# Deformable-convolution block: values and their transposes in three places, two PSUM banks for transposed values, one for the shuffle

## What is computed

```python
x = x + _L0_conv_ref(_gn(x), L0_conv_W, L0_conv_b)      # 8 groups, 3x3, then per group (channels, pixels) -> (pixels, channels)
x = x + _L1_conv_ref(_gn(x), ...)
# _L1_conv_ref:
out = relu(_bn(_conv1x1(x, conv1_w, conv1_b), ...))       # 512 -> 128 channels
offset = _conv3x3(out, off_w, off_b)                      # 18 channels: dy, dx for 9 taps
out = _deform_conv3x3(out, offset, dconv_w, dconv_b)      # val = v00*wy0*wx0 + v01*wy0*wx1 + v10*wy1*wx0 + v11*wy1*wx1
out = _bn(out, ...)
out = relu(_bn(_conv1x1(out, conv2_w, conv2_b), ...))     # 128 -> 512 channels
```

## Time and profile before

| | us |
|---|---|
| median of 3 runs | 2017.78 |
| lowest and highest run | 2017.04 and 2052.67 |
| the profiled execution | 2034.64 |
| its span, first to last instruction | 2032.8 |
| mean granted TensorE clock in it | 0.910 |
| DMA, mean over the span | 220 GB/s |

### The profile page before, as it was taken

The page is one execution under the profiler, slowest core; times in us unless marked ns, Lnnn a source line. Parts: engine busy times, 40 slices in busy tenths (PEclk is TensorE's granted clock), DMA queues, the critical chain, the costliest instruction groups (busy, mean ns, idle before and its releaser), DMA issues.

```text
span 2032.8 us, 30610 instructions
## 1 busy us (share of the span) xinstructions
PE 1658.7 (82%) x9504; PEld 794.9 (39%) x9504; DVE 1424.5 (70%) x3577; ACT 952.5 (47%) x1411; POOL 1198.0 (59%) x1160
## 2 busy tenths in 40 slices
PE   4888888888888888988887978888888888887555
PEld 2444434344443434434343433434334343433211
DVE  5547678686777778686776857777686777867553
ACT  6645445454545445454543636545354553523221
POOL 0036666665666666665665666666655665666762
PEclk9988889998998989899998989999999998998866
DMA  8267678697786868778686867969687786867774
GB/s 216 63 179 212 201 198 278 193 280 209 216 269 194 268 184 268 220 211 278 204 265 179 263 210 203 292 184 293 190 240 241 218 265 185 250 191 224 221 214 122
DMA packets 161423, 446.68 MB, mean 220 GB/s; under 512 B 26598, under 2 KB 27238, under 8 KB 161254
## 3 DMA queue, kind: packets, MB, share of 16 engines
q0 software_dynamic: 92160, 302.06, 51.0%
q1 hardware_dynamic: 69094, 142.58, 22.2%
HBM read 373.23 MB, written 71.30 MB: 219 GB/s over the span
## 4 chain that ended last, share of the span: by engine, by line
PE 42%; issue 20%; DVE 11%; another core or an unknown queue 10%; ACT 9%; DMA 4%; POOL 3%; SPq 1%; ACTq 0%; DVEq 0%; POOLq 0%
PE bank L820 18%; PE bank L797 7%; PE bank L788 4%; PE bank L805 3%; DVE sb_rows L601 3%; POOL sb_rows L364 3%; PE bank L910 3%; DMA sb_xc<-x 2%; DVE sb_val L609 2%; PE bank L852 2%; ACT sb_split L442 2%; DVE sb_split L641 2%; PE bank L836 2%; ACT sb_norm L429 2%
## 5 line engine op out<-in xcount | busy, mean ns | idle before, releaser
L364 POOL DMA_INDIRECT sb_rows<-table,sb_ridx x1152 | 1194.2, 1037 | 784.1 <-issue 441.6
L820 PE MATMUL bank<-sb_split,sb_wg 128*64 128x512 f16 x4608 | 630.7, 406 | 101.6 <-issue 85.8
L601 DVE SCALAR_TENSOR_TENSOR sb_rows<-sb_rows,sb_frac 128x256 f32<-128x256 f32 x1152 | 500.4, 480 | 186.5 <-DMA sb_rows<-table,sb_ridx 139.4
L820 PEld LDWEIGHTS bank<-sb_split,sb_wg 128*64 128x64 f16 x4608 | 266.2, 114 | 434.8 <-issue 270.7
L609 DVE SCALAR_TENSOR_TENSOR sb_val<-sb_rows,sb_frac 128x128 f32<-128x128 f32 x1152 | 328.7, 347 | 29.1 <-PE bank L788 11.0
L797 PE MATMUL bank<-sb_valT,sb_wd 128*128 128x512 f32 x576 | 342.9, 679 | 7.4 <-issue 7.0
L788 PE MATMUL bank<-sb_eye_sb,sb_val 128*128 128x128 f32 x1152 | 200.9, 300 | 146.7 <-ACT sb_valT L392 72.6
L392 ACT ACTIVATE sb_valT<-bank 128x512 f32<-128x512 f32 x288 | 174.0, 604 | 228.4 <-remote 133.3
L414 ACT ACTIVATE sb_conv_sb<-bank,sb_bias 128x512 f32<-128x512 f32 x128 | 147.0, 1149 | 226.4 <-remote 130.1
L788 PEld LDWEIGHTS bank<-sb_eye_sb,sb_val 128*128 128x128 f32 x1152 | 132.7, 150 | 307.3 <-issue 255.9
L403 ACT ACTIVATE sb_res<-bank,sb_bn_t,sb_bn_s 128x512 f32<-128x512 f32 x128 | 99.5, 778 | 297.4 <-remote 175.6
(11 more groups left out here) (76 smaller groups left out, 1067.4 us busy)
## 6 DMA issues: line engine op xcount, KB each, us to landing
table<-sb_table_sb SPq DMA_DIRECT2D x144, 256.0 KB
sb_xc<-x SPq DMA_DIRECT2D x64, 512.0 KB
sb_xl<-x SPq DMA_DIRECT2D x128, 256.0 KB
out<-sb_xl SPq DMA_DIRECT2D x128, 256.0 KB
sb_rows<-table,sb_ridx POOLq DMA_INDIRECT x1152
sb_rows<-w_group SPq DMA_DIRECT2D x8, 288.0 KB, 9.6
sb_wd<-w_def SPq DMA_DIRECT2D x1, 576.0 KB
sb_w<-w_in SPq DMA_DIRECT2D x1, 512.0 KB
```

Of the source, the lines that this page charges most:

```text
L364: pool.indirect_dma_start(out=rows[:, (c % RING) * PER + i, :], out_offset=None, in_=tables[u % 2], in_offset=bass.IndirectOffsetOnAxis(ap ...
L601: op = nc.vector.scalar_tensor_tensor(r[:, 0:2 * CH], r[:, 2 * CH:4 * CH], frac[:, parity, half * PER + i, k, 0:1], r[:, 0:2 * CH], ALU.mu ...
L820: op = nc.tensor.matmul(pair_ps[half][64 * e:64 * e + 64, :], wg[:, 2 * q + e, k, part * GIN:(part + 1) * GIN], plane(split1[:, 2 * q + e, ...
```

## The change

- `val` and `valT` get three places in place of two (`VALUES`). `value_out` waits for the `deform` of one chunk further back, and VectorE's second interpolation for the transposes of one chunk further back.
- Transposed values alternate between banks 4 and 5. `transpose_values` of chunk c waits for the copy of chunk c-2 in place of c-1.
- Both parts of the shuffle use bank 2. A part waits until the part before it has been added.
- Table tiles alternate between bank 2 and `out_ps`. Tile 0 waits for both parts of the next image's first shuffle, tile 1 for the last `relu_out` of the image before the last; the first `out_conv` of an image waits for the copies of all tiles.

```diff
+    VALUES = 3
...
-        val = sb("val", [128, 2, PER * CH], f32)
-        valT = sb("valT", [128, 2, HALF], f32)
+        val = sb("val", [128, VALUES, PER * CH], f32)
+        valT = sb("valT", [128, VALUES, HALF], f32)
...
-        shuf_ps = (banks[2], banks[5])
+        shuf_ps = banks[2]
...
-        valT_ps = banks[4]
+        valT_ps = (banks[4], banks[5])
         def_ps = banks[6]
         out_ps = banks[7]
+        table_ps = (shuf_ps, out_ps)
...
             def value_out(image, c):
                 act.wait_ge(valT_done, count(CHUNKS, image, c + 1))
-                act.wait_ge(def_done, count(CHUNKS, image, c - 1))
-                nc.scalar.activation(valT[:, c % 2, :], valT_ps[:, :], ACT.Copy).then_inc(val_out, 1)
+                act.wait_ge(def_done, count(CHUNKS, image, c - VALUES + 1))
+                nc.scalar.activation(valT[:, c % VALUES, :], valT_ps[c % 2][:, :], ACT.Copy).then_inc(val_out, 1)
...
-                    nc.scalar.activation(table_sb[:, m % TBUFS, :], shuf_ps[m % 2][:, :], ACT.Copy).then_inc(tile_out, 1)
+                    nc.scalar.activation(table_sb[:, m % TBUFS, :], table_ps[m % 2][:, :], ACT.Copy).then_inc(tile_out, 1)
...
-                    dve.wait_ge(valT_done, count(CHUNKS, image, c - 1))
+                    dve.wait_ge(valT_done, count(CHUNKS, image, c - VALUES + 1))
...
             def transpose_values(image, c):
                 pe.wait_ge(val_done, count(CHUNKS, image, c + 1))
-                pe.wait_ge(val_out, count(CHUNKS, image, c))
+                pe.wait_ge(val_out, count(CHUNKS, image, c - 1))
...
-            def out_conv(image, g):
+            def out_conv(image, g, table):
                 if g == 0:
+                    if table:
+                        pe.wait_ge(tile_out, count(TILES, image + 1, TILES))
                     pe.wait_ge(d_out, count(2, image, 2))
...
             def shuffle(image, q, part):
                 pe.wait_ge(conv_out, count(2 * QUADS, image, 2 * q + 2))
-                pe.wait_ge(mid_done, count(2 * QUADS, image, 2 * q + part - 1))
+                pe.wait_ge(mid_done, count(2 * QUADS, image, 2 * q + part))
...
                 def table_tile(m):
                     if m < 2:
-                        pe.wait_ge(mid_done, count(2 * QUADS, nxt, m + 1) if a2 else count(2 * QUADS, t, 2 * QUADS))
+                        if m == 0:
+                            pe.wait_ge(mid_done, count(2 * QUADS, nxt, 2) if a2 else count(2 * QUADS, t, 2 * QUADS))
+                        else:
+                            pe.wait_ge(relu_done, count(GROUPS, t - 1, 0))
```

More of the change, by code:

```diff
@@ L609, in interpolate @@
                         op = nc.vector.scalar_tensor_tensor(
-                            val[:, c % 2, i * CH:(i + 1) * CH], r[:, CH:2 * CH],
+                            val[:, c % VALUES, i * CH:(i + 1) * CH], r[:, CH:2 * CH],
                             frac[:, parity, half * PER + i, k, 1:2], r[:, 0:CH], ALU.mult, ALU.add)
@@ L650, in add_shuffled @@
                     dst = xl[:, buf, 2 * q:2 * q + 2, part * (HALF // 2):(part + 1) * (HALF // 2)]
-                    nc.vector.tensor_tensor(dst, shuf_ps[part].rearrange("p (e n) -> p e n", e=2), dst, ALU.add)\
+                    nc.vector.tensor_tensor(dst, shuf_ps.rearrange("p (e n) -> p e n", e=2), dst, ALU.add)\
                       .then_inc(mid_done, 1)
@@ L785, in transpose_values @@
                 pe.wait_ge(val_done, count(CHUNKS, image, c + 1))
-                pe.wait_ge(val_out, count(CHUNKS, image, c))
+                pe.wait_ge(val_out, count(CHUNKS, image, c - 1))
                 for i in range(PER):
-                    op = nc.tensor.transpose(valT_ps[:, i * CH:(i + 1) * CH],
-                                             val[:, c % 2, i * CH:(i + 1) * CH], eye_sb[:, :])
+                    op = nc.tensor.transpose(valT_ps[c % 2][:, i * CH:(i + 1) * CH],
+                                             val[:, c % VALUES, i * CH:(i + 1) * CH], eye_sb[:, :])
                 op.then_inc(valT_done, 1)
@@ L796, in deform @@
                     pe.wait_ge(d_out, count(2, image, half))
-                nc.tensor.matmul(def_ps[:, :], wd[:, k * CH:(k + 1) * CH], valT[:, c % 2, :], start=k == 0,
+                nc.tensor.matmul(def_ps[:, :], wd[:, k * CH:(k + 1) * CH], valT[:, c % VALUES, :], start=k == 0,
                                  stop=k == TAPS - 1).then_inc(def_done, 1)
-            def out_conv(image, g):
+            def out_conv(image, g, table):
                 if g == 0:
+                    if table:
+                        pe.wait_ge(tile_out, count(TILES, image + 1, TILES))
                     pe.wait_ge(d_out, count(2, image, 2))
@@ L829, in shuffle @@
                 pe.wait_ge(conv_out, count(2 * QUADS, image, 2 * q + 2))
-                pe.wait_ge(mid_done, count(2 * QUADS, image, 2 * q + part - 1))
+                pe.wait_ge(mid_done, count(2 * QUADS, image, 2 * q + part))
                 if q == 1 and part == 0:
                     pe.wait_ge(tile_out, count(TILES, image - 1, TILES))
-                dst = shuf_ps[part].rearrange("p (e j o) -> p j e o", e=2, o=GIN)
+                dst = shuf_ps.rearrange("p (e j o) -> p j e o", e=2, o=GIN)
                 for jj in range(COLS // 4):
@@ L909, in table_tile @@
                     for i, src in enumerate((h_sb[:, r], dx[:, r], dy[:, r], dxy[:, r])):
-                        op = nc.tensor.transpose(shuf_ps[m % 2][:, i * CH:(i + 1) * CH], src, eye_sb[:, :])
+                        op = nc.tensor.transpose(table_ps[m % 2][:, i * CH:(i + 1) * CH], src, eye_sb[:, :])
                     op.then_inc(tile_done, 1)
@@ L964, in step @@
                     if tail and s in OUT_CONV:
-                        out_conv(t - 1, OUT_CONV[s])
+                        out_conv(t - 1, OUT_CONV[s], b)
                     offsets_and_table(s, 3)
```

## The result

| | before | changed |
|---|---|---|
| median, lowest, highest (us), 4 runs each | 2035.16, 2017.04, 2052.67 | 2047.19, 2046.90, 2057.41 |
| the profiled execution, its span | 2034.64, 2032.8 | 2047.11, 2045.3 |
| mean granted clock in it | 0.910 | 0.914 |

The ratio is 1.016 with an interval of 1.0107 to 1.0213. I had forecast 1996.8 us, 21 us less than the 2017.78 of before, in a range of 1964 to 2038. The changed kernel lies outside it, on the slower side, though still within the 2%. The kernel before took 2017 us twice and 2052 us twice (the table ahead of the prediction has three of these four), and the ratio leaves out the two of 2052 us as executions in a slower state of the chip. So 1.6% rests on two runs of the kernel before; the means over all four and four, 2035.0 and 2049.7 us, are 0.7% apart.

The account below looks back on a forecast made before the run. The prediction took queue handovers, chiefly TensorE's transposes waiting for ScalarE's copy with VectorE ahead, to bound the kernel. Won 39 less lost 18 gave net 21 us, from 2017.78 to 1996.8 us, range 1964 to 2038.

Parts of the forecast that it names:

- won 39: Sum of the gains expected from doubling the bank of the transposed values: 8 + 18 + 8 + 5 us.
- The transposes' wait goes: TensorE's value transposes (L788) would lose their idle time for the copy L392: 59.0 us steady, 72.6 in all.
- Slot 1, won 8: Transposes and part of the offset convolution run inside the gap behind ScalarE's DMA wait: 0 to 18 us, taken 8.
- Slots 7 and 9, won 18: Transposes there wait less, since a group convolution stands between them and `deform`: 8 to 26.8 us, taken 18.
- The merged bank, lost 10 and 4: Shuffle parts wait for VectorE's add: 10 us in slot 11, 4 at the start, nothing in the other four slots.
- Start and end, won 5: Waits for the copy outside the steady stretch, 13.6 us in all, shrink: 0 to 14 us, taken 5.
- The third place for values, nothing: A third place for `val` lets VectorE, already ahead, get further ahead, hidden behind TensorE's work: no time.
- Clock, won 8, lost 4: Closed gaps in slots 7 and 9 give back clock, 0 to 15 us; longer shuffle gaps cost 0 to 10.
- The tiles in `out_ps`, nothing: Table tiles keep their two-bank alternation in bank 2 and `out_ps`: no time; 11 us if cover were gone.
- the rule: A skill's report that a second PSUM buffer gave no further gain (126.6 to 125.5 us); by it, gains about nothing.
- No change: Rival: TensorE passes the transposes and stops at ScalarE's next product; 2012 to 2022 us, say 2017; chance 0.25.
- The slower rival: At the merged shuffle bank, each of five handovers an image shows one VectorE add: about 2060 us; chance 0.15.

Follow-up runs that it names:

- the pair with half the gathers: Kernel before and changed kernel, each with only the first two of four gathers a chunk issued after the first three chunks: 1691.14 and 1685.30 us.
- The pair with half the shuffle: Kernel before without the second part of every shuffle, tiles in bank 2 and `out_ps`, with one or two banks for transposed values: 2034.42 and 2031.68 us.
- three other orders: Two VectorE adds earlier in the changed kernel, 1.0152; in the kernel before, value transposes behind the second convolution, 1.0094, or a ScalarE copy ahead of a ReLU, 0.9981.
- the larger sets: The unedited changed kernel measured again against the kernel before, on two chips: 2037.57 us, ratio 1.0061, and 2031.90 us, ratio 1.0043.
- the earlier pace: Kernel before with GpSimd's wait for the transposes ahead of a chunk's second gather instead of its third: 2017.94 us, ratio 0.9967.

## Why the prediction was wrong

The step that failed is the one from waits to time: "won 39" priced the waits for the copy at their length. Where only the doubling differs and no bank is merged, 79.8 us of these waits went and the time moved by 0.5 us by the means, with a standard error of 3.1, and by 2.7 us by the medians. Term by term:

**The transposes' wait goes** (my first step). Right: 72.6 us to nothing.

**Slot 1, won 8.** Wrong size. The mechanism was named, that the tile stops behind the same DMA, and I still took two thirds of a microsecond a step for it. Measured: 62.7 against 60.9 us in slots 1 and 2, nothing won that stands out of the scatter.

**Slots 7 and 9, won 18.** The gaps before the transposes shrank by 17 us, as counted, but 27.3 us stand before the shuffle of slot 9. I had read there that the add ended 1.4 us ahead, and called four of the five handovers "hidden as long as TensorE doesn't gain more than that". TensorE now stood there up to 5.2 us for the add.

**The merged bank, lost 10 and 4.** This term was mis-sized. The gaps are 13.4 us in slot 11, priced at 10, and 9.2 us in the first 100 us, priced at 4; slots 9 and 16, priced at nothing, have 27.3 and 13.5. What ended with the add is 57.0 us in all (34.2 and 34.5 in the two later traces of the changed kernel). Its effect on the time is smaller than on the waits: the kernel with only that edit has 22.9 us of such waits and is slower by 0.15%, with its interval on both sides of nothing.

**Start and end, won 5.** Not seen. From slot 1 of the last step in the steady stretch to the end it is 388.7 us before and 396.1, 393.0 and 394.1 in three traces of the changed kernel, and 379.7 to 397.4 in six other kernels with one bank. Only the pair with half the gathers shows it clear of that: some 6 us longer, not shorter.

**The third place for values, nothing, since VectorE is ahead.** Here the premise failed. The earlier trace rows gave 2.6 us of waits for the values against 59.0 for the copy, and I took the small number for a lead. A wait that ends last hides how late the others were. With the copy out of the way the values were just behind: 34.6, 44.4 and 30.9 us of waits in three traces, 19.8 before (10.7 to 27.7 in six other kernels with one bank), and 44.6 against 26.2 in the pair with half the gathers. The pair with half the shuffle does not show it (37.3 with one bank, 29.4 with two), so it was not always VectorE that came next.

**Clock, won 8, lost 4.** Not seen: the granted clock was 0.910 before and 0.914, 0.926 and 0.908 in three traces of the changed kernel, its busy TensorE 1670.0, 1645.9 and 1671.5 us against 1658.7.

**The tiles in `out_ps`, nothing.** Right, 0.9993.

**The sum.** Its common error lies under all terms: I took a microsecond of a TensorE wait for a microsecond of time. The runs say that in this kernel it isn't. TensorE with some 40 us less work, VectorE with 222 us less, half the gathers' bytes and three other orders moved the time by -17 to +15 us, far less than what was taken away. What moves it much is GpSimd's gathers: 328 us less with half of them, 195 us more with the same number and no pacing. The page has 1152 of them at 1037 ns with 0.30 us between two, about 1540 us of work, which I passed over because "59%" leaves those 0.30 us out. The timeline of the changed kernel shows a run of eight, with what the others do meanwhile:

```profile
373.25 0.95 POOL L366 DMA_INDIRECT sb_rows<-table,sb_ridx  x1 [2.40 <-remote]
...
379.12 0.60 PE L840 MATMUL bank<-sb_eye_sb,sb_conv_sb 128*128 128x128 f32 x4
...
382.56 0.95 POOL L366 DMA_INDIRECT sb_rows<-table,sb_ridx  x1 [0.30 <-issue]
382.66 0.31 PE L790 MATMUL bank<-sb_eye_sb,sb_val 128*128 128x128 f32 x1
383.36 0.32 PE L790 MATMUL bank<-sb_eye_sb,sb_val 128*128 128x128 f32 x1 [0.39 <-issue]
...
384.79 1.15 ACT L416 ACTIVATE sb_conv_sb<-bank,sb_bias 128x512 f32<-128x512 f32 x1 [5.90 <-remote]
384.91 0.69 DVE L653 TENSOR_TENSOR sb_xl<-bank,sb_xl 128x512 f32<-128x512 f32 x1 [3.27 <-remote]
385.60 0.94 POOL L366 DMA_INDIRECT sb_rows<-table,sb_ridx  x1 [2.10 <-PE bank L790]
```

GpSimd issues from 373.25 to 383.51 without a pause. TensorE's shuffle is recorded at 379.12, its signal reaches VectorE at 384.91, 1.4 us after the last gather, together with that for ScalarE; 0.7 us later GpSimd itself gets the release that it stands for. The four transposes between, ready to run as far as the trace tells, start 0.7 us apart. In the kernel before, 128 such waits of ScalarE and VectorE last over 1 us (100 to 1950 us), and 102 of them end over 0.8 us behind the last gather, with none running, which is 13% of that time. GpSimd's pauses of over 0.6 us add up to 384 us before and 381, 343 and 362 us in the three traces after: the change moved them little, and the time with them.

The late signals were in front of me: the 3.33 us "<-remote" of the earlier trace rows, of which the prediction said that it couldn't read the cause and that the change doesn't touch it. The change does touch it. It puts a handover through VectorE into TensorE's queue, and each handover needs one of those signals. "VectorE's adds follow TensorE's own signals, so they move with it", the reason by which I kept the merged bank's rival small, holds for the products and not for the signals. The stops of 1.05 us in the earlier trace rows, which I took for late instructions, are "issue" rows too: before the group convolution they are 85.8 us in the kernel before and 16.3 with two gathers, so they also go with the gathers. Whether they are instructions on their way, no run shows.

**The rivals and the rule.** "No change" had named the mechanism (TensorE stops at the next product) and looked for it on ScalarE's side; most of it came from VectorE. Its 2017 us were nearer than my 1996.8. The slower rival's 2060 us are nearer still to the 2047 of the first set, by luck: the larger sets, at 0.4 and 0.6% over the kernel before, stand with "no change", and the bank alone showed 3 us. The rule of the Trainium skill, TensorE: Matmul & The Clock Gate, HAM oscillation, by which a second PSUM buffer gave one kernel no further gain, agrees with this case: 2034.42 to 2031.68 us with the merged bank out of the way, where 0.3% is less than the scatter. I had set it aside for rows that count waits.

**What stays open.** Whether the doubling costs beside one shuffle bank, and why (8 and 9 us by the medians on two chips, clear of the scatter only on the second), when it costs none without it: the totals of waits differ among executions by more than that. That gathers hold back TensorE's signals is inferred from when they arrive, from the kernel without the pace and from that with two gathers; what in the chip they share was not tried. Of the 328 us, the share of GpSimd's own time and that of the late signals were not told apart.

No kernel that does the whole work was faster than the kernel before by more than the scatter. That kernel stands, with the earlier pace at 0.9967 no more than a candidate.

## What to carry to other kernels

Before you price a wait at its length, take work away from each engine and see whether the time moves; here a wait of 73 us left and 69 us of waits for another engine came. The count of waits for a releaser shows who came last, not how far ahead the others are. Add the fixed gap between instructions to an engine's busy share (59% was over 75%), and when many engines wait for releases that the trace doesn't name, lay the moments at which these arrive beside the rows of every other engine; here they came in GpSimd's pauses.

## What the runs showed of the hardware

Back-to-back gathers of GpSimd go with late signals of TensorE: 790 us of unnamed waits with four gathers a chunk, 28 us with two, 988 us with four and no pacing (spans 2032.8, 1692.2 and 2218.6 us), and 734 us with four of half the bytes. TensorE's own stops for "issue" go with them too, 177 us against 24 with two. With two gathers TensorE's same products took 1531.5 us at a granted clock of 0.974 instead of 1658.7 at 0.910. A gather of half the bytes held GpSimd as long as a whole one, 1048 ns against 1037, and 0.30 us stood between two of a run in both. The kernel before gave medians of 2019 to 2025 us on three chips and 2041 us on a fourth, so that only runs of one set could be compared.
